# Two-layer transformer block on one core: first experts' weights split during the cross attention, attention weights' low parts in a head's first step, first head's split moved and its zeroing left out

## The chip, the core and the metric

The kernel runs on one core of a Trainium2 chip. A core has five engines that run their own instruction streams and meet on semaphores: TensorE (PE, matrix products into PSUM), VectorE (DVE), ScalarE (ACT), GpSimd (POOL) and SyncE (SP, here only a queue that issues transfers). The metric is the device time of one launch in microseconds, lower is better.

## What is computed

2048 tokens of width 256 (32 sequences of 64) pass six blocks, each with a layer norm ahead and added to the residual `x`:

```
x = x + L0_attn(norm(x))              # rotary recurrence, 6 heads
x = x + L0_xattn(norm(x), ctx, mask)  # grouped-query cross attention, 16 heads, ALiBi, mask
x = x + L0_ffn(norm(x))               # 16 routed experts, top 2, and 2 shared ones; itself x + shared + routed
x = x + L1_attn(norm(x))              # lightning attention, 16 heads of 128
x = x + L1_xattn(norm(x), ctx)        # attention with quantised q, k, v and weights
x = x + L1_ffn(norm(x))               # 16 routed experts, top 4, and a shared one
```

The cross attention takes, per head, `softmax(q k / 4 + slope * (key - query position), masked)` times `v`. An expert of L0_ffn is `w2(gelu(g x + gb) * (w1 x + b1)) + b2`. The lightning attention projects q, k, v (SiLU) and a gate (sigmoid) per head, multiplies `q k^T` with a decay that stays inside 64-token sequences here, multiplies with `v`, normalises over all heads, gates and projects out.

## The kernel before

The functions run one behind the other, each as one or a few blocks of five engine streams; a block ends when all five have ended. Tokens lie in 16 tiles of 128 (`NT`); a step of most loops handles 512 tokens (`BLK`), so four steps (`NBLK`) make a pass, of four tiles each (`TPB`). Nothing plans the order: every engine's stream is written out by hand, and semaphores tie them.

**Products in two halves.** To have near-float32 products at 16-bit speed, operands are split into a high part (`x * 1024` rounded to float16) and a low part (what the rounding left), and `split_product` (L117) runs high*high, high*low and low*high. So every weight and every activation needs a high part (an ACT instruction with `scale=SPLIT`) and a low part (a subtraction on DVE or POOL).

**`layernorm`** (L159 on). DVE computes moments, ACT the root (L221, with a load of ACT's function table ahead), DVE normalises the tiles (L205), PE turns them (L246), ACT copies them from PSUM (with `split` as high parts, L228), and DVE makes the low parts (L197). With `scalar_first` ACT does something of the caller's ahead of the root, with `gpsimd` POOL beside it all.

**`gqa_cross_attention`** (L538 on). Per block of 512 tokens PE projects queries, keys (and values from `ctxS`, a copy of the block's context that POOL makes, L598); ACT copies them out. Then four steps of one tile n: PE's scores (L704); DVE scales them and adds the bias (L658), takes the maximum (L663) and subtracts it (L664, two inputs in SBUF), ACT takes the exponential (L631), DVE sums (L679) and inverts, PE turns the weights (L752), ACT copies them (L634, two per step), PE multiplies with the values (L762), DVE divides (L684), PE turns and projects out (L722), DVE adds to X (L669). POOL makes the next bias (ALiBi plus mask, 128x1024, L602) in the one of two buffers that step n-2 has consumed: it waits for `biased >= n + 1` and nothing else.

**`experts_top2`** (L1117 on). Stage of its own (`m.stage()`): its semaphores are cleared at its end. `RowNorm` normalises on DVE (L900), adds to X (L905), ACT makes high parts (L916) and DVE low parts (L892); for each 512 tokens SP then issues a transposing transfer (L925, output in `xh` or `xl`) and a transfer that keeps the rows in DRAM. PE computes the router's logits (L117), ACT the scores (L996), and a chain of some 80 DVE instructions chooses two experts per token and places the tokens (`Dispatch`, L1009 to L1114). Then POOL gathers the rows of 12 groups of 512 places from DRAM (L1247), SP transposes them (L1214), PE runs them through their experts, ACT and DVE evacuate, the results are kept and gathered back (L1255) into `G`, and DVE combines them (L1360); the shared experts run on PE meanwhile.
The weights of the 18 experts are loaded by SP in six slots (`weights`, L1178 to L1186) and split here: ACT scales them in place (L1263, L1264) and rounds them (L1266, L1267), POOL subtracts (L1237, L1238). ACT's split of experts 0 and 1 stands ahead of the root, those of 2 to 5 between the high parts, the rest before and behind the scores. The first routed product waits for all 18 (`split`).

**`lightning_attention`** (L1501 on). Its norm is `layernorm(..., split=True, scalar_first=first_high, gpsimd=first_low)`: ACT scales head 0's weights in place and rounds them (two instructions of 128x1280, L1577 and L1579), POOL zeroes `SQ` (L1582), subtracts (L1584) and zeroes `ACC` (L1585). Then 16 heads of four steps s. In a step PE runs, for step s+1, the projections, and for step s `k q`, the previous step's output product and `A v`; ACT evacuates; DVE masks (`mask`, L1684), adds the previous output from PSUM to `ACC` (`add`, L1692), gates (L1698) and makes y's low part (L1701); POOL squares (L1604) and sums the squares in `SQ` (L1607). The next head's weights are rounded by ACT in step 0 (L1619) and subtracted by DVE behind step 1:

```
for q in range(SPH):
    s = h * SPH + q
    mask(s, h)
    if not (first and q == 0):
        add(s - 1, (q - 1) % SPH)
    gated(s, h, q)
    if q == 1 and not last:
        weights_low(h + 1)
```

SP then issues one transposing transfer of both parts (`turn`, L1559) into `T`, and the loads of the head after. PE waits for that transposition in step 3, ahead of the next head's first projection (`pe.wait_ge(wt_in, 16 * (h + 2))`).

## Time and profile before

| | us |
|---|---|
| Median of three runs | 2724.72 (2721.74 to 2728.42) |
| Profiled execution, its own time | 2709.75 |
| Its span | 2707.9 |

| Engine | busy us | share | instructions |
|---|---|---|---|
| PE | 1998.0 | 74% | 15918 |
| DVE | 1845.4 | 68% | 3197 |
| ACT | 1458.6 | 54% | 2020 |
| POOL | 1018.0 | 38% | 921 |

| Stage | from, us | to, us | granted PE clock |
|---|---|---|---|
| cross attention, steps | 279.3 | 477.9 | 0.77 |
| experts' router | 477.9 | 551.1 | 0.51 |
| experts' products, combination | 551.1 | 716.2 | 0.88 |
| norm ahead of the lightning attention | 716.2 | 744.7 | 0.56 |
| lightning attention | 744.7 | 1320.9 | 0.98 |
| quantised attention | 1320.9 | 2200.5 | 0.56 |
| top-4 experts | 2200.5 | 2707.9 | 0.96 |

Times count from the start of the span. The granted clock is a share of 2.4 GHz. Engines overlap, so busy times are no sum of anything: what counts is what each stage waits for last. The chain of waits that the page follows back from the last instruction reaches only to the start of the last stage, so earlier stages are read from time lines. In these, a line is one instruction or a run of like ones; in brackets is how long its engine had been idle, and whose work ended that.

### The profile page before, as it was taken

The numbers are of one execution on the slowest core, as the hardware profiler recorded it, in microseconds if no ns is written. First come the engines' busy times: TensorE is split into PE (matmuls) and PEld (weight loads), VectorE is DVE, ScalarE is ACT, GpSimd is POOL, SyncE is SP. The second block draws the span as 40 slices with busy tenths as digits, with TensorE's granted clock in tenths as the row PEclk, the third lists the DMA queues.
The fourth block names the chain that finished last, engine by engine and source line by source line (L and its number), as shares of the span: only waits on it lengthen the run. The fifth ranks groups of instructions, "written<-read, shape, count | busy, mean of one in ns | idle before, by whom it ended". The sixth has DMA issues, their size and how long they took to land. (4 is left out here: it accounts for less than half of the span.)

```text
span 2707.9 us, 44268 instructions
## 1 busy us (share of the span) xinstructions
PE 1998.0 (74%) x15918; PEld 1185.8 (44%) x15918; DVE 1845.4 (68%) x3197; ACT 1458.6 (54%) x2020; POOL 1018.0 (38%) x921
## 2 busy tenths in 40 slices
PE   6884777158399999999563566666666549999998
PEld 3332555146267677777452122222222324444444
DVE  5997566733645455555656999999999546666665
ACT  4662333523254444444232888888888326666664
POOL 0000221553423333333134788888888401001010
PEclk8886777579799999999776555555555659999999
DMA  3000000666311111111000556565666200000001
GB/s 93 0 0 21 1 0 0 170 147 146 82 23 37 39 39 39 39 39 30 24 0 0 102 106 108 108 106 108 107 107 108 44 19 18 17 26 17 26 17 40
DMA packets 416195, 145.93 MB, mean 54 GB/s; under 512 B 359021, under 2 KB 412997, under 8 KB 416069
## 3 DMA queue, kind: packets, MB, share of 16 engines
q1 hardware_dynamic: 412229, 133.76, 24.2%
q0 software_dynamic: 3840, 10.49, 1.7%
q8 instruction: 79, 1.29, 0.2%
q14 instruction: 47, 0.39, 0.0%
HBM read 47.69 MB, written 10.49 MB: 21 GB/s over the span
## 5 line engine op out<-in xcount | busy, mean ns | idle before, releaser
L2057 POOL CAST xnT<-xl 128x2048 bf16<-128x2048 uint8 x256 | 483.6, 1890 | 16.1 <-DMA xl<-xh 0.7
L2092 PE MATMUL psum<-e_KT,e_QT 48*128 48x512 bf16 x1024 | 265.1, 618 | 271.9 <-DVE ctxT L2125 125.1
L2125 DVE TENSOR_SCALAR_CACHE_REDUCE ctxT<-psum,e_nsq 128x1024 f32<-128x1024 f32 x256 | 314.7, 1282 | 11.8 <-PE psum L2092 10.1
L2125 DVE TENSOR_SCALAR_CACHE_REDUCE e_Smore<-psum,e_nsq 128x1024 f32<-128x1024 f32 x256 | 314.7, 1282 | 1.4
L2143 ACT ACTIVATE xh<-e_Smore,e_ebias 128x2048 uint8<-128x2048 f32 x128 | 256.3, 2002 | 48.4 <-POOL e_ebias L2064 48.4
L2143 ACT ACTIVATE xh<-ctxT,e_ebias 128x2048 uint8<-128x2048 f32 x128 | 256.3, 2002 | 47.5 <-POOL e_ebias L2064 47.5
L1604 POOL TENSOR_TENSOR d_sq<-d_oS 128x512 f32<-128x512 f32 x64 | 96.9, 1514 | 399.1 <-ACT d_oS L1653 399.1
L117 PE MATMUL psum<-xh,d_T 128*128 128x512 f16 x768 | 221.9, 385 | 22.8 <-DMA d_T<-d_Ws 19.0
L2092 PEld LDWEIGHTS psum<-e_KT,e_QT 48*128 48x128 bf16 x1024 | 33.9, 107 | 401.8 <-DVE ctxT L2125 190.4
L2281 POOL TENSOR_TENSOR f_WA<-f_W,f_WA 128x512 f16<-128x512 f32 x17 | 19.6, 1155 | 410.0 <-ACT f_W2H L2301 410.0
L2102 PEld LDWEIGHTS psum<-e_Vi,xnT 128*128 128x128 bf16 x4096 | 119.3, 104 | 112.9 <-issue 104.3
L117 PE MATMUL psum<-xh,f_WA 128*128 128x512 f16 x544 | 154.5, 387 | 13.9 <-DVEq L2336 11.8
L2352 DVE SCALAR_TENSOR_TENSOR X<-psum,f_route,X 128x256 f32<-128x256 f32 x272 | 112.8, 477 | 70.3 <-PE psum L2412 70.3
L1701 DVE SCALAR_TENSOR_TENSOR d_yl<-d_y,d_nw,d_yh 128x512 f16<-128x512 f32 x64 | 105.4, 1647 | 72.0 <-ACT d_yh L1658 72.0
L2412 PE MATMUL psum<-f_W2H,f_hh 128*128 128x256 f16 x544 | 151.1, 278 | 3.1 <-DVE f_hh L2364 3.1
L2412 PE MATMUL psum<-f_W2L,f_hh 128*128 128x256 f16 (+1 forms) x544 | 151.0, 278 | 0.0
L2102 PE MATMUL psum<-e_Vi,xnT 128*128 128x16 bf16 x4096 | 131.2, 175 | 8.1 <-POOL xnT L2057 8.1
L1628 ACT ACTIVATE d_gt<-psum 128x512 f32<-128x512 f32 x64 | 38.2, 597 | 164.1 <-PE psum L117 164.1
L2315 ACT ACTIVATE f_h<-psum 128x512 f32<-128x512 f32 x68 | 40.6, 597 | 158.0 <-PE psum L117 158.0
L2342 DVE TENSOR_TENSOR f_pr<-psum,f_h 128x512 f32<-128x512 f32 x68 | 47.0, 692 | 111.3 <-ACT f_h L2315 111.3
L1698 DVE SCALAR_TENSOR_TENSOR d_y<-d_gt,d_oS 128x512 f32<-128x512 f32 x64 | 44.3, 692 | 108.3 <-ACT d_oS L1653 108.3
L117 PE MATMUL psum<-xl,d_T 128*128 128x512 f16 x384 | 116.2, 385 | 0.0
(366 smaller groups left out, 4806.8 us busy)
## 6 DMA issues: line engine op xcount, KB each, us to landing
kept_y<-c_y SPq DMA_DIRECT2D x12, 512.0 KB, 3.7
d_Wn<-in_L_attn_w_qkv SPq DMA_DIRECT2D x16, 384.0 KB, 3.4
f_W<-in_L_ffn_w_routed SPq DMA_DIRECT2D x32, 176.0 KB, 2.5
xl<-xh SPq DMA_TRANSPOSE x256, 3.1
ctx_rows<-in_ctx SPq DMA_DIRECT2D x1, 2048.0 KB, 9.3
X<-in_x SPq DMA_DIRECT2D x1, 2048.0 KB, 14.7
c_Wgu<-in_L_ffn_rg SPq DMA_DIRECT2D x16, 128.0 KB, 2.6
c_Wgu<-in_L_ffn_rw SPq DMA_DIRECT2D x16, 128.0 KB, 2.7
```

The source lines that it names most:

```text
L117: mm = pe.matmul(out, lhsT(a, k), rhs(b, k), start=(n == 0), stop=(n == len(terms) - 1))
L1604: pool.tensor_tensor(sq[:, :], o, o, ALU.mult).then_inc(squared, 1)
L1698: dve.scalar_tensor_tensor(y[:, :], gt[:, q % 2, :], 1.0, oS[:, q % 2, :], ALU.add, ALU.mult).then_inc(yready, 1)
L1701: dve.scalar_tensor_tensor(yl[:, :], y[:, :], nw[:, ds(h, 1)], yh[:, :], ALU.mult, ALU.subtract).then_inc(ysplit, 1)
L2057: pool.tensor_copy(PT[:, sl, :], P8[:, sl, :, :].rearrange("p c q -> p (c q)").bitcast(U8)).then_inc(unpacked, 1)
L2092: mm = pe.matmul(m.bank[pair_banks(c + odd) + q], QT[rows, n // 2, :], KTt[rows, n % H // 2, col:col + BLK], start=True, stop=True)
L2102: mm = pe.matmul(m.bank[6 + j // 8][:, j % 8 * HD:(j % 8 + 1) * HD], PT[:, n % SLOTS, k // 2 * 2 * P + k % 2:(k // 2 + 1) * 2 * P:2], Vi[: ...
L2125: dve.tensor_scalar(S32[sl][:, hf * HALF:(hf + 1) * HALF].rearrange("p (a b) -> p a b", a=2), m.psum[:, b:b + 2, :], nsq[:, n + odd:n + od ...
L2143: act.activation(e8[:, sl, :], S32[sl], ACT.Exp, bias=ebias[:, sl:sl + 1], scale=-1.0, accum_out=esum[:, n:n + 1]).then_inc(exped, 1)
L2342: dve.tensor_tensor(pr[:, st % 2, 0, :], m.bank[1][:, :], h1[:, st % 2, 0, :], ALU.mult).then_inc(product, 1)
L2352: last = dve.scalar_tensor_tensor(m.X[:, t, :], m.bank[4 + 2 * (q % 2) + j // 2][:, (j % 2) * D:(j % 2 + 1) * D], R.route[:, t, ds(e, 1)], ...
L2412: mm = pe.matmul(m.bank[4 + 2 * (q % 2) + j // 2][:, (j % 2) * D:(j % 2 + 1) * D], a, b, start=(n == 0), stop=(n == len(terms) - 1))
```

## The change

- `SplitWeights` (new) holds the experts' weight slots (four), the split weights and their semaphores. The two shared experts are loaded during the cross attention's norm and split ahead of its loop; the 16 routed ones are split one per step of the loop, ACT's part behind its copies of the step, POOL's part ahead of the bias. SP reloads a slot when POOL has done with it. `experts_top2` has no weight work left. Both functions are in one `m.stage()`.
- In the cross attention the biases of tiles 0 and 1 are made ahead of the loop, and step n makes that of tile n+2; two more rows of `neg`, set to zero, stand for tiles 16 and 17, whose biases nobody reads. The copy `ctxS` moves from POOL to ACT.
- In the router ACT's second to fourth high parts stand behind the wait for the eleven small loads. The gathered results go to `m.xnT` in sixteen slots instead of eight.
- In the lightning attention's norm ACT takes the root first and then rounds head 0's weights in one instruction (`scalar_mid`); DVE makes the low part between the normalisation and the low part of the norm's second block (`vector_mid`), in one instruction for scale and subtraction. POOL has nothing there.
- `ACC` and `SQ` are not zeroed: the first four sums are copies, head 0's squares are written straight to `SQ`.
- `weights_low(h + 1)` moves from behind step 1's `gated` to the first step, between `add` and `gated`.

```
+                    if vector_mid and b == 1:
+                        vector_mid(dve)
...
-                if scalar_first:
-                    scalar_first(act)
                 act.wait_ge(moments_done, (r + 1) * (NT + 1))
                 act.activation(sd[:, :], mom[:, :, 1], ACT.Sqrt, bias=eps[:, :]).then_inc(sd_done, 1)
+                if scalar_mid:
+                    scalar_mid(act)
...
+    def load(self, sp, kind, e, slot):
+
+        for part, name in enumerate(("g", "w1")):
+            sp.dma_start(self.Wgu[:, slot, :, part, :],
+                         self.w[f"L0_ffn_{kind}{name}"][e].rearrange("(k p) f -> p k f", p=P)).then_inc(self.w_in[slot], 16)
+        sp.dma_start(self.Wd[:, slot, :], self.w[f"L0_ffn_{kind}w2"][e]).then_inc(self.w_in[slot], 16)
+
+    def scalar(self, act, e, slot, loads, n):
+
+        act.wait_ge(self.w_in[slot], 48 * loads)
+        act.activation(self.Wgu[:, slot], self.Wgu[:, slot], ACT.Copy, scale=SPLIT)
+        act.activation(self.Wd[:, slot], self.Wd[:, slot], ACT.Copy, scale=SPLIT).then_inc(self.scaled, 1)
+        act.wait_ge(self.scaled, n + 1)
+        act.activation(self.Wx[:, ds(e, 1), 0].rearrange("p o k a f -> p (o k a f)"),
+                       self.Wgu[:, slot].rearrange("p k a f -> p (k a f)"), ACT.Copy)
+        act.activation(self.WdH[:, ds(e, 1)].rearrange("p o d -> p (o d)"), self.Wd[:, slot], ACT.Copy).then_inc(self.high, 1)
+
+    def gpsimd(self, pool, e, slot, n):
+
+        pool.wait_ge(self.high, n + 1)
+        flat = lambda x: self.Wx[:, ds(e, 1), x].rearrange("p o k a f -> p (o k a f)")
+        pool.tensor_tensor(flat(1), self.Wgu[:, slot].rearrange("p k a f -> p (k a f)"), flat(0), ALU.subtract)
+        pool.tensor_tensor(self.WdL[:, ds(e, 1)].rearrange("p o d -> p (o d)"), self.Wd[:, slot],
+                           self.WdH[:, ds(e, 1)].rearrange("p o d -> p (o d)"), ALU.subtract).then_inc(self.split, 1)
...
+            for slot in range(W.SH):
+                W.load(sp, "s", slot, slot)
...
+                    sp.wait_ge(W.split, slot + 1)
+                    W.load(sp, "r", slot, slot)
+                for slot in range(W.SH, W.SLOTS):
+                    W.load(sp, "r", slot, slot)
+                with sp.Fori(1, NBLK) as i:
+                    for slot in range(W.SLOTS):
+                        sp.wait_ge(W.split, i * W.SLOTS + (W.SH - W.SLOTS + 1) + slot)
+                        W.load(sp, "r", i * W.SLOTS + slot, slot)
+
             @block.gpsimd
             def _(pool):
-                pool.wait_ge(prep, 1 + KC * C)
+                for slot in range(W.SH):
+                    W.gpsimd(pool, W.NE + slot, slot, slot)
+                pool.wait_ge(prep, 2 + KC * C)
+
+                def mask_bias(n, half):
+                    pool.wait_ge(biased, n + 1)
+                    pool.tensor_tensor(bias[:, half, :, :], alibi[:, :, :],
+                                       neg[:, ds(n, 1), :].broadcast_to((P, NH, SEQ)), ALU.add).then_inc(bias_ready, 1)
+
+                mask_bias(0, 0)
+                mask_bias(1, 1)
                 with pool.Fori(0, NBLK) as i:
-                    pool.wait_ge(proj, i * 4 + 4)
-                    pool.tensor_copy(ctxS[:, :, :], m.ctxT[:, :, ds(i * BLK, BLK)]).then_inc(ctx_copied, 1)
                     for tt in range(TPB):
-                        n = i * TPB + tt
-                        pool.wait_ge(biased, n + 1)
-                        pool.tensor_tensor(bias[:, tt % 2, :, :], alibi[:, :, :],
-                                           neg[:, ds(n, 1), :].broadcast_to((P, NH, SEQ)), ALU.add).then_inc(bias_ready, 1)
+                        W.gpsimd(pool, i * W.SLOTS + tt, tt, i * W.SLOTS + (W.SH + tt))
+                        mask_bias(i * TPB + (tt + 2), tt % 2)
...
+                    W.scalar(act, W.NE + slot, slot, 1, slot)
+                act.wait_ge(prep, 2 + KC * C)
                 with act.Fori(0, NBLK) as i:
+                    act.wait_ge(proj, i * 4 + 4)
+                    act.activation(ctxS[:, :, :], m.ctxT[:, :, ds(i * BLK, BLK)], ACT.Copy).then_inc(ctx_copied, 1)
...
+                        W.scalar(act, i * W.SLOTS + tt, tt, i + (2 if tt < W.SH else 1), i * W.SLOTS + (W.SH + tt))
...
+                dve.memset(neg[:, NT:, :], 0.0).then_inc(prep, 1)
...
-    STAGES, GOT, TURNED, GSLOTS = 6, 2, 3, 8
+    GOT, TURNED, GSLOTS = 2, 3, 16
...
-        G = norm.xn[:, :, :, :].rearrange("p a b d -> p (a b) d")
+        G = m.xnT[:, :, :].rearrange("p a b -> p (a b)").rearrange("p (s d) -> p s d", s=GSLOTS)
...
-                    for n in range(STAGES):
-                        weights(n)
...
-                split_high(0)
-                split_high(1)
                 norm.scalar_sd(act)
-                for b in range(NBLK):
-                    norm.scalar_high(act, b)
-                    split_high(2 + b)
-                split_high(STAGES)
-                split_high(STAGES + 1)
+                norm.scalar_high(act, 0)
                 act.wait_ge(loaded, 16 * NLOADS)
                 act.activation(b2[:, 0, :], b2[:, 0, :], ACT.Copy, scale=HS * SPLIT).then_inc(bias_high, 1)
                 R.scalar_gate(act, R.wa[:, :, :].rearrange("p k e -> p (k e)"))
+                for b in range(1, NBLK):
+                    norm.scalar_high(act, b)
                 R.scalar_scores(act, m.bank[6])
-                for n in range(STAGES + 2, NE + SH):
-                    split_high(n)
...
-                pe.wait_ge(split, NE + SH)
...
-            act.activation(flat(Wn[:, :, :]), flat(Wn[:, :, :]), ACT.Copy, scale=SPLIT).then_inc(wscaled, 1)
-            act.wait_ge(wscaled, 1)
-            act.activation(flat(Ws[:, 0]), flat(Wn[:, :, :]), ACT.Copy).then_inc(whigh, 1)
-
-        def first_low(pool):
-            pool.memset(SQ[:, :], 0.0).then_inc(squared, 4)
-            pool.wait_ge(whigh, 1)
-            pool.tensor_tensor(flat(Ws[:, 1]), flat(Wn[:, :, :]), flat(Ws[:, 0]), ALU.subtract).then_inc(wsplit, 1)
-            pool.memset(ACC[:, :, :], 0.0).then_inc(acc_zero, 1)
-
-        layernorm(nc, m, preload, split=True, scalar_first=first_high, gpsimd=first_low)
+            act.activation(flat(Ws[:, 0]), flat(Wn[:, :, :]), ACT.Copy, scale=SPLIT).then_inc(whigh, 1)
+
+        def weights_low(dve, h):
+
+            dve.wait_ge(whigh, h + 1)
+            dve.scalar_tensor_tensor(flat(Ws[:, 1]), flat(Wn[:, :, :]), SPLIT, flat(Ws[:, 0]), ALU.mult,
+                                     ALU.subtract).then_inc(wsplit, 1)
+
+        layernorm(nc, m, preload, split=True, scalar_mid=first_high, vector_mid=lambda dve: weights_low(dve, 0))
...
-                with pool.Fori(0, NH) as h:
+                for q in range(SPH):
+                    pool.wait_ge(ocopied, q + 2)
+                    pool.tensor_tensor(SQ[:, q * BLK:(q + 1) * BLK], oS[:, q % 2, :], oS[:, q % 2, :],
+                                       ALU.mult).then_inc(squared, 2)
+                with pool.Fori(1, NH) as h:
...
-                def add(s, q):
+                def add(s, q, fresh):
                     dve.wait_ge(outs, s + 2)
                     for half in range(2):
                         t = q * TPB + 2 * half
                         a2 = ACC[:, t:t + 2, :].rearrange("p t d -> p (t d)")
-                        last = dve.tensor_tensor(a2, m.bank[6 + half][:, :], a2, ALU.add)
+                        if fresh:
+                            last = dve.tensor_copy(a2, m.bank[6 + half][:, :])
+                        else:
+                            last = dve.tensor_tensor(a2, m.bank[6 + half][:, :], a2, ALU.add)
...
-                        if not (first and q == 0):
-                            add(s - 1, (q - 1) % SPH)
+                        if n or q:
+                            add(s - 1, (q - 1) % SPH, n * SPH + q <= SPH)
+                        if q == 0 and not last:
+                            weights_low(dve, h + 1)
                         gated(s, h, q)
-                        if q == 1 and not last:
-                            weights_low(h + 1)
...
-                dve.wait_ge(acc_zero, 1)
-                head(0, True, False)
-                with dve.Fori(1, NH - 1) as h:
-                    head(h, False, False)
-                head(NH - 1, False, True)
+                head(0, 0, False)
+                head(1, 1, False)
+                with dve.Fori(2, NH - 1) as h:
+                    head(h, 2, False)
+                head(NH - 1, 2, True)
...
+        with m.stage(), ExitStack() as split:
+            W = SplitWeights(m, w, split)
+            gqa_cross_attention(nc, m, w, W)
+            experts_top2(nc, m, w, W, kept_rows, kept_y)
...
```

## Rows read from the trace of the kernel before

**Rows 1.** Windows view, lightning attention: engines' busy us, granted PE clock, DMA share.

```profile
744.70:1320.90 576.20, 546.48 (x4512) 404.25 (x4512) 304.66 (x358) 256.32 (x420) 178.41 (x128) 0.98 0.15 33
```

**Rows 2.** Time line of DVE, cross attention: start us, us, instruction, idle before, releaser.

```profile
292.98 1.29 DVE L658 SCALAR_TENSOR_TENSOR b_S<-psum,b_bias 128x512 f32<-128x512 f32 x2 [12.15 <-PE psum L704]
...
303.27 2.32 DVE L664 TENSOR_TENSOR b_S<-b_S,b_mx 128x1024 f32<-128x1024 f32 x1
...
321.93 1.22 DVE L679 TENSOR_REDUCE b_tot<-b_S 128x16 f32<-128x1024 f32 x1 [0.46 <-ACT b_S L631]
...
461.24 1.22 DVE L679 TENSOR_REDUCE b_tot<-b_S 128x16 f32<-128x1024 f32 x1 [0.46 <-ACT b_S L631]
...
467.70 1.22 DVE L679 TENSOR_REDUCE b_tot<-b_S 128x16 f32<-128x1024 f32 x1 [0.46 <-ACT b_S L631]
```

**Rows 3.** Time lines of POOL and ACT, the same stage.

```profile
302.16 2.35 POOL L602 TENSOR_TENSOR b_bias<-b_alibi,b_neg 128x1024 f32<-128x1024 f32 x1 [5.37 <-DVE b_S L658]
...
301.02 0.60 ACT L634 ACTIVATE b_PT<-psum 128x512 f32<-128x512 f32 x1 [0.26 <-PE psum L752]
```

**Rows 4.** Split of an expert's weights: ACT time line, POOL source line (ns min/median/max).

```profile
523.08 0.61 ACT L1263 ACTIVATE c_Wgu<-c_Wgu 128x512 f32<-128x512 f32 x1
...
524.87 0.61 ACT L1263 ACTIVATE c_Wgu<-c_Wgu 128x512 f32<-128x512 f32 x1
...
L1237 POOL TENSOR_TENSOR c_Wx<-c_Wgu,c_Wx x18: 1147/1189/3194, 483.9 to 546.4; 128x512 f16<-128x512 f32 x18
```

**Rows 5.** Time lines of DVE, SP and PE, router of the first experts.

```profile
487.28 0.25 DVE L887 RECIPROCAL c_rstd<-c_sd 128x16 f32<-128x16 f32 x1 [2.67 <-ACT c_sd L912]
...
494.88 1.93 SPq L925 DMA_TRANSPOSE xh<-xnT  x1
...
506.88 3.02 SPq L925 DMA_TRANSPOSE xl<-xnT  x1
...
516.91 0.81 PE L117 MATMUL psum<-c_wa,xl 128*128 128x16 f16 x24 [1.97 <-DMA xl<-xnT]
```

**Rows 6.** Lines view of DVE, 525.8 to 550.2 us: xcount, busy us, mean ns, idle.

```profile
L1100 DVE TENSOR_TENSOR c_y<-c_iota,c_row 128x2048 f16<-128x2048 f32 x2 | 6.0, 2993 | 0.0
...
L1096 DVE TENSOR_TENSOR c_tilehot<-c_iota,c_tile 128x768 f16<-128x768 f32 x2 | 3.3, 1632 | 0.0
...
L1070 DVE TENSOR_SCALAR c_tile<-c_slot 128x32 f32<-128x32 f32 x1 | 1.1, 1137 | 0.0
```

**Rows 7.** Time lines, norms: cross attention's (270.36), then lightning attention's.

```profile
270.36 2.67 DVE L205 TENSOR_SCALAR ln_xn<-X,ln_mom,ln_rstd 128x256 f32<-128x256 f32 x8
...
721.75 1.17 DVE L188 BATCH_NORM_AGGREGATE ln_mom<-ln_stats 128x2 f32<-128x6 f32 x16
...
726.55 6.60 DVE L205 TENSOR_SCALAR ln_xn<-X,ln_mom,ln_rstd 128x256 f32<-128x256 f32 x8
...
727.24 3.51 POOL L1585 MEMSET d_ACC<- 128x4096 f32 x1
...
731.91 3.67 PE L246 MATMUL psum<-ident,ln_xn 128*128 128x128 f32 x16 [31.57 <-DVE ln_xn L205]
```

**Rows 8.** Time lines, lightning attention: PE at head boundaries, DVE in head 1.

```profile
779.14 0.61 PE L117 MATMUL psum<-xh,d_T 128*128 128x512 f16 x2 [2.02 <-DMA d_T<-d_Ws]
...
1267.64 0.61 PE L117 MATMUL psum<-xh,d_T 128*128 128x512 f16 x2 [1.22 <-DMA d_T<-d_Ws]
...
794.14 1.29 DVE L1692 TENSOR_TENSOR d_ACC<-psum,d_ACC 128x512 f32<-128x512 f32 x2 [0.51 <-PE psum L117]
...
797.13 0.69 DVE L1698 SCALAR_TENSOR_TENSOR d_y<-d_gt,d_oS 128x512 f32<-128x512 f32 x1 [1.69 <-ACT d_oS L1653]
...
805.44 0.69 DVE L1698 SCALAR_TENSOR_TENSOR d_y<-d_gt,d_oS 128x512 f32<-128x512 f32 x1 [1.69 <-ACT d_oS L1653]
...
808.85 1.48 DVE L1707 SCALAR_TENSOR_TENSOR d_Ws<-d_Wn,d_Ws 128x1280 f16<-128x1280 f32 x1
```

More of the change, by code:

```diff
@@ L535, in _, with __init__, gqa_cross_attention @@
                 output(NBLK - 1)
-def gqa_cross_attention(nc, m, w):
+class SplitWeights:
+    NE, SH, F, SLOTS = 16, 2, 128, 4
+    def __init__(self, m, w, own):
+        NE, SH, F, SLOTS = self.NE, self.SH, self.F, self.SLOTS
+        self.w = w
+        self.Wgu = m.sb("c_Wgu", [P, SLOTS, KC, 2, F], ctx=own)
+        self.Wd = m.sb("c_Wd", [F, SLOTS, D], ctx=own)
+        self.Wx = m.sb("c_Wx", [P, NE + SH, 2, KC, 2, F], F16, own)
+        self.WdH, self.WdL = (m.sb("c_" + n, [F, NE + SH, D], F16, own) for n in ("WdH", "WdL"))
+        self.scaled, self.high, self.split = (m.sem(f"c_{n}") for n in ("scaled", "high", "split"))
+        self.w_in = [m.sem(f"c_w{i}") for i in range(SLOTS)]
+    def load(self, sp, kind, e, slot):
[17 more added lines that the diff above has]
+                           self.WdH[:, ds(e, 1)].rearrange("p o d -> p (o d)"), ALU.subtract).then_inc(self.split, 1)
+def gqa_cross_attention(nc, m, w, W):
     G, C, HD = 4, 4, 16
@@ L1233, in _ @@
                 pool.memset(b2r[:, :, :], 0.0).then_inc(bias_clear, 1)
-                for n in range(NE + SH):
-                    e, slot = ORDER[n], n % STAGES
-                    pool.wait_ge(high, n + 1)
-                    pool.tensor_tensor(Wx[:, e, 1], Wgu[:, slot], Wx[:, e, 0], ALU.subtract)
-                    pool.tensor_tensor(WdL[:, e], Wd[:, slot], WdH[:, e], ALU.subtract).then_inc(split, 1)
                 pool.wait_ge(norm.kept, 16 * NBLK)
@@ L1716, in finish, with head @@
                         dve.scalar_tensor_tensor(m.X[:, t, :], ACC[:, t, :], rstd[:, t:t + 1], m.X[:, t, :], ALU.mult, ALU.add)
-                def head(h, first, last):
+                def head(h, n, last):
                     for q in range(SPH):
```

69 lines of the change are left out of this document (16 added, 53 removed).

## Prediction

> **What bounds the kernel now.** The program is seven stages one behind the other, so I read the busy times by stage first, then the time lines of the stages that the diff touches, for what each waits on last. In the lightning attention TensorE (PE) is busy 546 of 576 us at nearly full clock [rows 1]: only idle time of PE can be won there. The cross attention is a ring of VectorE (DVE), ScalarE (ACT) and PE, some 7.6 us a step, but 6.46 us (461.24 to 467.70) in the last ones, where GpSimd (POOL) has nothing left to do [rows 2]. The router of the first experts is a DVE chain with SyncE's (SP's) transpositions in it [rows 5, 6], and the norm ahead of the lightning attention waits for DVE [rows 7].
>
> **What one lock does.** POOL's bias ran from 302.16 to 304.51 [rows 3]; DVE's subtraction, asked for at 303.27, took 2.32 us [rows 2], which is the remaining 1.24 us plus the 1.22 us that 1024 elements take (the sum at 461.24 [rows 2]), less some overlap. So a DVE instruction with two SBUF inputs and a POOL instruction exclude each other. DVE's reductions and its reads of PSUM did not stretch. All terms below use this.
>
> **1. Cross attention, given 18 expert splits.** One split is 1.79 us of ACT (523.08 to 524.87) and 1.81 us of POOL: 1.15 for 512 elements [rows 4] and 0.66 at that rate for the down part's 256. ACT's copies end at 301.62 [rows 3] and its next exponential waits for the subtraction that ends at 305.59 [rows 2]: 4.0 us free, which cover the 1.79 (without them, every step would pay 1.79). The context copy that ACT takes over, at most 1.2 us by the 0.60 of half its size [rows 3], comes while PE still computes the block's queries. The six loads ahead of the stage ride on SP behind those of the norm; the later ones have a whole block each. The DVE memset of 128 elements is 0.1 us by size. POOL's order changes: bias n+2 now stands behind split n, and split n behind the exponentials' transposed copies on ACT. Worked through a block of four steps, from its first score:
> - step 0: POOL is idle at the first subtraction, so that takes 1.22, not 2.3 us: 1.1 us gained.
> - step 1: ACT's copies ended 1.65 us before the subtraction began [rows 2, 3]; plus 1.79, POOL's split is ready 0.15 us after that start, waits for its 1.22, runs 1.81, then the bias 2.35 [rows 3]: ready 5.4 us after the start. DVE wants it after 3.9 (1.22 plus exponential, sum and reciprocal). So 1.1 us gained, 1.5 lost.
> - steps 2 and 3: the subtraction meets one half of the split instead of the bias, about 0.4 to 1 us, and the bias is just about in time.
> The sum is 27.4 us from first score to last exponential, against 28.95 now (292.98 to 321.93 [rows 2]): -1.55 in three blocks. In the last block two subtractions already run free, 26.7 (28.95 less twice 1.1), and would now meet POOL: +0.7. Together **-4.0**. No row shows the new interleaving; its bounds are -15, fourteen stretches of 1.1 gone and no bias late, and +20, the first rival. I take the value worked out, since one lock at a time is what rows 2 and 3 show.
>
> **2. Router.** The 72 ACT and 36 POOL instructions of the splits leave. (a) The square root stood behind two splits and a table load: DVE waited 2.67 us for it [rows 5]; some 0.35 remain, -2.3. With POOL quiet DVE then needs 1.34 us for four normalisations (2.67 for eight [rows 7]), 1.2 each for the addition and the low part, so the first low part ends at 491.6 where its transposition is now issued at 494.88 [rows 5]: -3.3. From there to the last landing at 516.91 [rows 5] are 22.0 us, with six weight loads on SP just ahead of the third transposition at 506.88 [rows 5]. Without them and with DVE's spacing of 3.7, 3.7, 3.7 and 1.2 us the landing comes at 508.5: **-8.4**. Bounds: -6.8, where the transfers keep their present spacing less 3.5 us for six issues, and -8.9, where they follow DVE at once; I take the inner value because the transfer engines then carry nothing else. ACT now waits for the eleven small loads ahead of the second high part; they are the first things that SP issues, from 478 on at about half a microsecond each, and are wanted at 489. If they came late, everything above would slip by as much.
> (b) Behind the scores DVE works 24 us beside POOL's splits. The two of 2048 elements took 2.99 each [rows 6]; free they take 2.28 (0.69 us for 512 [rows 8] and 1.22 for 1024 [rows 2] give 1.04 ns an element): -1.4. The two of 768 took 1.63, free 0.96: -1.35. A 32-element operation took 1.14 [rows 6] and needs 0.18 by the same line: -0.96. Seven more groups of that view by the same comparison: -4.9. Together **-8.6** (bounds -4.5 and -9.5). The gathers, the routed loop (PE waiting on transposed rows) and the combination keep their lengths and shift; sixteen gather slots for eight are worth 0.5 us of POOL waits at most, taken as 0. Router: **-17.0**.
>
> A page can be held against (a): "DMA: Bandwidth & Descriptors" of the Trainium skill, section Latency and other measured facts, gives a transposition 261 GB/s, by estimate 2.0 us for a block's 512 KB; the blocks would then follow DVE's low parts directly, and the term would be -17.5. No row here isolates it.
>
> **3. Norm ahead of the lightning attention.** Moments are ready at 722.92, but the first of eight normalisations begins at 726.55, behind two ACT passes over the head's weights and a table load [rows 7]. Afterwards the root comes first and they begin at 723.6: -3.0. They then took 6.60 us because POOL's split and the zeroing of 3.51 us ran to 730.75; free, eight take 2.67 [rows 7]. The first transposition starts at 731.91 [rows 7] and would start at 725.0: **-6.9**. The moved low part (1.48 us on DVE [rows 8]) runs from 726.35 to 727.85, before the first PSUM low part can start at 728.2, and the weights' transposition is issued 0.5 us later than now against a start of PE that comes 6.9 earlier: by my estimate 3 us are left. ACT's one pass instead of two fits behind the root. The two memsets cost nothing except as lockers. Bounds -3.0 (only the earlier start) and -7.5.
>
> **4. Low part in a head's first step.** Now it is made in the second step, at 808.85 [rows 8], and PE waits for the transposition at every head boundary. From the stall before 779.14 to the one before 1267.64 [rows 8] are 488.5 us for fourteen heads; steps within a head are 8.31 us (797.13 to 805.44 [rows 8]), so 56 steps are 465.4: 23.1, plus the first stall's 2.02: **-25.1**. This includes the boundaries where PE resumed at the lower clock. One step earlier is 8.3 us, more than the 2.02 of the first stall and the 1.22 of the last [rows 8]. The price is DVE's place between the addition, which ends at 795.43, and the gate at 797.13 [rows 8]: 1.70 us free for 1.48, so nothing, with 0.2 us to spare. ACT's high part is made in that same first step already, ahead of the gate's input, and SP's transposition and three loads move forward with the low part. If ACT's part were late, DVE would wait ahead of the gate, and PE's output product behind it. PSUM copies instead of additions in the first four sums and POOL's single multiplication in head 0 run beside PE. Bounds: -25.5, and -4 if all DVE time is paid (second rival).
>
> **Sum:** -4.0 - 17.0 - 6.9 - 25.1 = -53.0 us. The profiled execution took 2709.75 us (2656.8 after); the median of the runs is 2724.72, 15 us above it, spread over stages that I can't see; I put the difference on the median: 2671.7 us.
>
> **Rivals.**
> - *POOL's instructions in a row keep DVE out until all are through.* For it: the eight normalisations of 6.60 us lost both POOL instructions in turn [rows 7]. Then subtractions 2 and 3 wait 4 us, a block grows by 4.5 us and the last by 6.7: +20 instead of -4, total -29: 2696. Against it: DVE waited for one bias only. 12%. The Trainium skill's "SBUF — State Buffer", section Who interferes with whom, says that whichever instruction starts first holds the shared ports for its whole length and the other blocks: by that the wait is one instruction, and the forecast stands. By that rule, the trace agrees on 303.27.
> - *The low part ahead of the gate delays it*: the 0.2 us are not there, and 1.4 us are paid at fifteen heads: -53 + 21, 2693. Against it: PE has its own work queued. 8%.
> - *The router's transfers were the bound*: only the contention term and the first 3.3 us come, -48: 2677. 5%.
> - *Slower: the lightning attention, no longer interrupted, loses PE's granted clock.* A step of 8.31 us would take 16.6 at 1.2 GHz; from about 7.4 such steps on the 53 us are gone and 8.2 more. For it: the stalls are PE's only pauses. Against it: 0.98 of full clock over the stage as it is, 95% busy [rows 1]. 2%; at ten steps 2755.
> - The change does not do what it says (the bias chain binds each step, no stall disappears): 1%.
>
> **Chances.** The forecast 72%. 0.3% is 8.2 us, about what a measurement of this kernel can tell from no change. The range: downward the bounds added as independent ones give -64, nearly all of it the cross attention's, and the runs differ by some 3 us, 2658; upward it takes in the terms' own bounds and the third rival and stops at the second, -33, leaving the first out: 2692. Faster 0.95, within 0.3% 0.03, slower 0.02.
>
> **What would show it.** After: DVE's normalisation in one run of 2.7 us in the third norm and no POOL work beside it; no wait of PE for the weights' transposition, heads of 33.2 us; scores 8 us and token list 17 us nearer to the router's start; in the cross attention stretched subtractions of at most about 2.4 us and waits for the bias in step 2 of a block. Wrong would be: a step over 8 us there, a PE wait for the low part of y in first steps, a transposition that still lands 22 us after the first, or a clock below 0.95 in the lightning attention.

## The result, and where the time went

The changed kernel takes 2679.58 us (median of 4 runs, 2676.91 to 2685.68) against 2725.01 (4 runs, 2721.74 to 2728.42): 0.983 of before, 95% interval 0.9812 to 0.9848, or -45.4 us. Forecast were 2671.7 us, 2658 to 2692. The sum of the terms is another matter, and the traces take it apart. Each row of this table is the distance between two marks on DVE's time line (its first instruction of a stage, the reading of the token list, the end of a stage's last addition into `X`), for the first profile of each kernel and for one more of each (a2 and a1 below):

| stretch, us | before | before, again | after | after, again |
|---|---|---|---|---|
| ahead of the cross attention's second norm | 263.2 | 261.3 | 262.8 | 263.7 |
| cross attention, from that norm | 214.9 | 214.9 | 208.0 | 208.0 |
| router, to the token list | 71.9 | 72.7 | 54.7 | 55.0 |
| experts' products and combination | 161.0 | 176.2 | 191.2 | 191.3 |
| gap to the next norm | 5.4 | 5.4 | 1.4 | 1.4 |
| norm ahead of the lightning attention | 28.3 | 27.8 | 21.4 | 21.5 |
| lightning attention | 576.2 | 574.4 | 555.0 | 555.4 |
| the rest | 1387.0 | 1387.1 | 1384.9 | 1384.3 |
| span | 2707.9 | 2719.6 | 2679.5 | 2680.5 |

Router and norm moved as forecast, the cross attention by more, and the experts' products, taken as unchanged, grew by 15 to 30 us. In no other profile of either kernel was this stretch as short as the 161.0 us of the first one of before; this is most of why the two first spans differ by only 28.4 us and the medians by 45.4.

**Cross attention.** The time line of DVE and POOL in step 1 of the first block of after (start us, us, instruction, idle before):

```profile
301.49 1.16 POOL L573 TENSOR_TENSOR c_Wx<-c_Wgu,c_Wx 128x512 f32 x1 [12.38 <-ACT c_WdH L567]
301.85 1.87 DVE L730 TENSOR_TENSOR b_S<-b_S,b_mx 128x1024 f32<-128x1024 f32 x1
302.60 1.65 POOL L574 TENSOR_TENSOR c_WdL<-c_Wd,c_WdH 128x256 f32 x1
304.21 2.36 POOL L655 TENSOR_TENSOR b_bias<-b_alibi,b_neg 128x1024 f32<-128x1024 f32 x1
306.70 1.29 DVE L724 SCALAR_TENSOR_TENSOR b_S<-psum,b_bias 128x512 f32<-128x512 f32 x2 [0.35 <-POOL b_bias L655]
```

The subtraction, asked for at 301.85, gets its 1.22 us once POOL's first half ends at 302.65. POOL's second half, next in its row, then waits for DVE: 1.65 us instead of the 0.66 by size. The lock goes to and fro, one instruction at a time. The bias is late, as worked out, but by 0.35 us here and by 1.46 to 1.49 in two steps of each later block; DVE's waits of the whole stage have one new row:

```profile
DVE b_S L724 <- POOL b_bias L655: 9.2, 7, 1.5
```

From first score to last sum a block takes 27.66, 27.60, 27.60 and 27.59 us, against 28.95, 28.92, 28.97 and 26.67 before: -3.1 in all, by hand -4.0. The other 4 us lie in the tails, where PE ends a block. The windows view over the start of the tails of blocks 1, 2 and 3 (granted clock is the last but two), first before, then after:

```profile
323.40:333.00 9.60, 8.87 (x45) 6.91 (x45) 1.31 (x4) 2.30 (x4) 0.00 (x0) 0.50 0.01 2
372.80:382.00 9.20, 8.47 (x49) 6.73 (x48) 1.12 (x3) 2.80 (x5) 0.00 (x0) 0.56 0.00 0
421.80:431.00 9.20, 8.37 (x43) 6.57 (x44) 1.29 (x4) 2.25 (x4) 0.00 (x0) 0.50 0.00 0
```

```profile
321.80:327.10 5.30, 4.76 (x44) 3.94 (x45) 1.24 (x4) 4.00 (x8) 4.48 (x4) 1.00 0.28 77
365.40:374.50 9.10, 8.37 (x48) 6.69 (x47) 0.95 (x4) 5.02 (x10) 4.09 (x3) 0.55 0.15 43
413.10:422.00 8.90, 8.17 (x48) 6.63 (x47) 0.94 (x3) 4.83 (x10) 4.09 (x3) 0.53 0.16 44
```

The same 44 or so matmuls keep PE busy for 8.2 to 8.9 us where the granted clock was at or near the lower level (0.50 to 0.56; 1.2 GHz) and for 4.8 at the full one (1.00; 2.4 GHz). The steps, shifted against the clock, met it in full once.

**Router.** SyncE's transpositions in after (the second number is what issuing one took on SyncE's queue, not the transfer), and PE's wait for the last:

```profile
484.31 2.06 SPq L991 DMA_TRANSPOSE xh<-xnT  x1
488.12 3.11 SPq L991 DMA_TRANSPOSE xh<-xnT  x1
491.94 3.41 SPq L991 DMA_TRANSPOSE xl<-xnT  x1
496.02 3.63 SPq L991 DMA_TRANSPOSE xl<-xnT  x1
```

```profile
501.43 0.81 PE L117 MATMUL psum<-c_wa,xl 128*128 128x16 f16 x24 [3.29 <-DMA xl<-xnT]
```

From first issue to last landing are 17.1 us, before 22.0 [rows 5]; the scores are complete 8.2 us nearer to the stage's start, forecast 8.4. Behind them the lines view of DVE has the group at its free size where before had 2993 and 1632 ns [rows 6]:

```profile
L1166 DVE TENSOR_TENSOR c_y<-c_iota,c_row 128x2048 f16<-128x2048 f32 x2 | 4.6, 2284 | 0.0
...
L1162 DVE TENSOR_TENSOR c_tilehot<-c_iota,c_tile 128x768 f16<-128x768 f32 x2 | 1.9, 956 | 0.0
```

That chain gave 9.0 us (forecast 8.6). The first three transpositions are issued within 0.1 us of DVE's low parts; the fourth, whose low part is ready at 493.05, only at 496.02, behind the third and its store. What held the transfers shows in the windows view from the first issue to the last landing, before and after (the last two numbers are the DMA engines' busy share and GB/s):

```profile
494.88:516.91 22.03, 2.09 (x72) 2.00 (x73) 14.37 (x22) 10.98 (x21) 10.00 (x11) 0.50 0.95 224
```

```profile
484.30:501.40 17.10, 2.26 (x72) 2.08 (x72) 10.53 (x22) 3.40 (x3) 0.00 (x0) 0.50 0.99 226
```

The DMA engines are full in both, at the same rate. By rate and length they moved some 4.9 MB before and 3.9 MB after, and at 225 GB/s this difference is worth about the 4.9 us that the stretch became shorter: the experts' weights no longer travel among the transpositions and the stores of the rows. From the first issue on the scores wait for these transfers, not for SyncE's issues or DVE's spacing. Over 485.6 to 488.0 only the first transposition's packets ran, at 208 GB/s with the engines full, and it landed 4.4 us after its issue. The Trainium skill, "DMA: Bandwidth & Descriptors", Latency and other measured facts, has 261 GB/s, by estimate 2.0 us for a block's 512 KB: this trace does not agree, by 208 GB/s they are 2.5 us.

**Norm ahead of the lightning attention.** The root first, then eight normalisations in 2.67 us, then the low part, all ahead of DVE's first PSUM low part; no POOL instruction beside them. Before, they began at 726.55 and took 6.60 [rows 7]. 6.9 us, as forecast:

```profile
724.67 0.31 ACT L221 ACTIVATE ln_sd<-ln_mom,ln_eps 128x16 f32<-128x16 f32 x1 [5.34 <-DVE ln_mom L188]
725.30 2.67 DVE L205 TENSOR_SCALAR ln_xn<-X,ln_mom,ln_rstd 128x256 f32<-128x256 f32 x8
727.89 1.48 DVE L1602 SCALAR_TENSOR_TENSOR d_Ws<-d_Wn,d_Ws 128x1280 f16<-128x1280 f32 x1
```

**Heads.** DVE's time line where a head's first step now holds the low part:

```profile
785.17 1.29 DVE L1716 COPY d_ACC<-psum 128x512 f32<-128x512 f32 x2 [0.62 <-PE psum L117]
786.37 1.48 DVE L1602 SCALAR_TENSOR_TENSOR d_Ws<-d_Wn,d_Ws 128x1280 f16<-128x1280 f32 x1
788.05 0.69 DVE L1724 SCALAR_TENSOR_TENSOR d_y<-d_gt,d_oS 128x512 f32<-128x512 f32 x1 [0.19 <-ACT d_oS L1676]
```

The gate still waits 0.19 us for ACT: these are the 0.2 us to spare that were forecast. PE's waits for the weights' transposition, 19.0 us in 15 pieces before, are gone: the waits view of PE over the stage has three rows, and none is a DMA. The windows view of the stage, against [rows 1]:

```profile
739.56:1294.57 555.01, 544.98 (x4512) 407.00 (x4512) 303.98 (x358) 256.50 (x420) 174.85 (x124) 0.98 0.15 35
```

Steps take 8.3 us throughout, and the 63rd step's gate comes 24.9 us earlier, counted from the stage's start (530.85 us against 555.74; forecast 25.1), or 23.1 against the second profile of before (553.96). The last step then takes 13.08 us instead of 9.32. What changed there, PE's 24 small matmuls for the first twelve tiles' norms, in before and in after:

```profile
1305.32 2.74 PE L1775 MATMUL psum<-d_ones,d_SQ 128*128 128x1 f32 x24
```

```profile
1275.72 5.12 PE L1796 MATMUL psum<-d_ones,d_SQ 128*128 128x1 f32 x24
```

Between the last steps PE idles for 2 us in both; in after the granted clock is down to 0.50 from about 1275 on, in before only from 1310. So the stage gave 21.1 us and not 24.9.

**Experts' products.** PE's waits by `issue` (it waited for nothing that the profile shows) over this stretch, before and after:

```profile
PE psum L1419 <- issue: 8.9, 10, 1.3
PE psum L117 <- issue: 0.2, 1, 0.2
```

```profile
PE psum L117 <- issue: 16.8, 26, 1.4
PE psum L1441 <- issue: 7.1, 10, 1.3
```

A sample from the shared products of after, PE and POOL: single matmuls some 0.7 or 1.4 us apart, for 16 us, while POOL issues one gather every 1.25 us without a pause. POOL stops at 681.4, and the stall ends 3 to 4 us later:

```profile
669.21 0.95 POOL L1292 DMA_INDIRECT xnT<-kept_y,c_home  x1 [0.30 <-issue]
670.08 0.27 PE L1443 MATMUL psum<-c_WdH,c_hl 128*128 128x256 f16 x1 [0.99 <-issue]
670.46 0.95 POOL L1292 DMA_INDIRECT xnT<-kept_y,c_home  x1 [0.30 <-issue]
670.79 0.27 PE L1444 MATMUL psum<-c_b2r,c_ones_bf 128*128 128x256 bf16 x1 [0.45 <-issue]
671.50 0.27 PE L1441 MATMUL psum<-c_WdH,c_hh 128*128 128x256 f16 x1 [0.44 <-issue]
...
680.48 0.95 POOL L1292 DMA_INDIRECT xnT<-kept_y,c_home  x1 [0.30 <-issue]
```

My theory was that PE's instructions come late while POOL issues gathers, and that sixteen slots, which let it issue twenty in a row, made it worse. The rivals: chance from run to run, or the code's new place. One row of the first profile of before already speaks against the simple form of this theory. There POOL issued all 32 gathers in a row, some 1.25 us apart:

```profile
668.21 0.95 POOL L1255 DMA_INDIRECT c_xn<-kept_y,c_home  x1 [31.47 <-DMA kept_y<-c_y]
...
707.68 0.94 POOL L1255 DMA_INDIRECT c_xn<-kept_y,c_home  x1 [0.30 <-issue]
```

and over 660 to 715 us, the shared products' part, PE has no wait by issue, only this row:

```profile
PE psum L1419 <- DVE c_hl L1334: 4.1, 3, 1.4
```

### The profile page after: what moved, and what is told of

Its sections match the earlier page's. It is cut to its first block and busy times, and to the rows that moved or that the text cites. A ratio compares the mean times of both kernels' runs of the same rounds, so it can differ in the third digit from the quotient of the medians.

```text
span 2679.5 us, 44374 instructions
## 1 busy us (share of the span) xinstructions
PE 2002.0 (75%) x15918; PEld 1190.3 (44%) x15918; DVE 1813.6 (68%) x3199; ACT 1461.2 (55%) x2023; POOL 1005.3 (38%) x912
## 5 line engine op out<-in xcount | busy, mean ns | idle before, releaser
L2302 POOL TENSOR_TENSOR f_WA<-f_W,f_WA 128x512 f16<-128x512 f32 x17 | 19.7, 1157 | 407.5 <-ACT f_W2H L2322 407.5
L573 POOL TENSOR_TENSOR c_Wx<-c_Wgu,c_Wx 128x512 f32 (+1 forms) x18 | 26.0, 1445 | 385.1 <-ACT c_WdH L567 385.1
```

## The experiments

### Both kernels once more (a1, a2)

No edit.

> The changed kernel, unaltered, for a second profile. In its first profile the first experts' products and combination (token list ready to the last addition into X) took 191.0 us against 160.8 before, with TensorE idle in pieces of some 0.7 us that no wait explains. Theory (the stalls are instruction delivery and differ from run to run): this stretch has another length here, anywhere from 160 to 190 us, and the span moves with it. Rival (the change itself lengthens it, by its sixteen gather slots or by the placing of its code): 191 us again, within 3 us. Time 2680 us, 0.983 of before, in both.

> The kernel before, unaltered, for a second profile. Its first profiled execution was 15 us faster than the median of its runs. Theory (run-to-run stalls in the first experts' products): this stretch takes 165 to 180 us instead of 160.8, and the span is some 2720 us. Rival (the stretch is fixed in each kernel): 161 us again and a span of 2708 us.

a1: 2676.09 us, 0.9811 of before (0.9788 to 0.9834), products and combination 191.3 us. a2: 2721.39 us in one run, 176.2 us. The stretch of after repeats within 0.1 us, so its growth is not chance: the rival held there. That of before moves by 15 us between two profiles: there the theory held.

### The change in two halves (a3, a4)

a3 is before with the hunks of the norm helper and the lightning attention; a4 is before with all the others.

> Only the last two parts of the change: the norm ahead of the lightning attention, and a head's low part in its first step with the first head's other engines. Prediction's terms: -6.9 and -25.1, less the 3.8 us that the clock took back at the lightning attention's end in the first profile of after: -28 to -32 us, 2693 to 2697 us. Rival (the parts help one another): less than 25 us.

> Only the first parts: the experts' weights split in the cross attention, the router without them, the gathers' sixteen slots. Prediction's terms: -4 and -17, and -3.4 measured besides in the first profile of after at the cross attention's and the stage's ends: -24 us, 2701 us. Rival (the change lengthens the experts' products by up to 30 us): between -24 and +6, the remainder of what a3 leaves of the whole -45: -13 to -17 us.

a3: 2698.69 us, 0.991 (0.9893 to 0.9928), -26.5 us, a little less than the 28 to 32 expected, though its last step took 9.32 us, the clock falling late as in before; a4's did too, so neither half's profile has the 3.8 us. a4: 2705.43 us, 0.9929 (0.9908 to 0.9949), -19.7 us: between the theory's 24 and the rival's 17. Products and combination took 184.8 us in a4 and 178.8 in a3. The halves add up to -46.2; the whole gave -45.4 in its first runs and -49.1 in those of a1.

### The gathers' slots (b1, b2)

```diff
-    GOT, TURNED, GSLOTS = 2, 3, 16
+    GOT, TURNED, GSLOTS = 2, 3, 8
-        G = m.xnT[:, :, :].rearrange("p a b -> p (a b)").rearrange("p (s d) -> p s d", s=GSLOTS)
+        G = norm.xn[:, :, :, :].rearrange("p a b d -> p (a b) d")
```

b1 is after with this edit, b2 is before with its reverse.

> The changed kernel with eight slots for the combination's gathers (in the norm's buffer, as before) in place of sixteen. Theory (TensorE's instructions come late while POOL issues gathers back to back, and sixteen slots let it issue twenty in a row): products and combination take 165 to 180 us instead of 185 to 191, no stall of TensorE of over 10 us in the shared products; time 2665 to 2672 us against 2676 to 2680. Rival (the slots have nothing to do with it): 185 to 191 us and 2680 us. Second rival (sixteen slots save POOL's waits, as intended): longer by 1 to 5 us.

> The kernel before with sixteen slots in place of eight, and nothing else. Theory (as for b1): products and combination take 180 to 190 us in place of the 161 to 179 of the profiles so far, with one stall of TensorE of 15 us or more in the shared products; 2730 to 2740 us. Rival: as before, 2725 us.

b1: 2670.80 us, 0.9802 (0.9785 to 0.9819); products and combination took 179.7 us, as expected. b2: 2727.85, 1.0017 (1.0005 to 1.0029), 5.0 us longer, so at the edge of what was expected; the stretch took 183.0 us. What they did is read best from the four additions of the shared products into X, here in b1:

```profile
654.93 1.29 DVE L1371 SCALAR_TENSOR_TENSOR X<-psum,X 128x512 f32<-128x512 f32 x2 [0.27 <-issue]
669.42 1.28 DVE L1371 SCALAR_TENSOR_TENSOR X<-psum,X 128x512 f32<-128x512 f32 x2
679.63 1.29 DVE L1371 SCALAR_TENSOR_TENSOR X<-psum,X 128x512 f32<-128x512 f32 x2 [0.27 <-PE psum L1444]
694.61 1.29 DVE L1371 SCALAR_TENSOR_TENSOR X<-psum,X 128x512 f32<-128x512 f32 x2 [7.46 <-remote]
```

First to fourth addition, in the profiles with gathers beside these products: sixteen slots 48.9, 48.2, 48.2, 47.4, 48.4 and 49.7 (after, a1, a4, b3, b4, c3) and 48.4 in b2, whose stage is otherwise that of before; eight slots 39.7, 39.3, 36.9 and 39.3 (b1, a2, a3, c1), and 28.0 in the first profile of before alone. So the slots cost some 9 us or more here, in either kernel, and the rest of the growth is not theirs. On the whole stage it is less: with sixteen the gap to the next norm is 1.3 to 1.4 us, with eight 5.4 to 5.6. Between the profiles of after and b1 3.7 us more lie in the last step of the lightning attention, which took 9.32 us in b1.

### All gathers behind the products (c2)

```diff
                 for sl in range(2):
                     pool.wait_ge(kept[sl], 16 * (QUADS // 2))
+                pool.wait_ge(summed, NBLK)
```

and DVE's additions of the gathered rows all behind its last shared addition.

> The changed kernel with all 32 gathers of the combination, and all its additions, behind the last shared product. Theory (the stall of TensorE in the shared products comes of the gathers that POOL issues beside them): no piece of TensorE idle by issue in that part; the last addition of a shared product comes 13 to 18 us earlier than in the two profiles of after, where it is bound by the stall. The whole is longer all the same, since 32 gathers take 40 us: products and combination 210 to 220 us. Rival (instruction delivery at that place of the code is slow whatever POOL does): the stall of 13 to 18 us is there, with no gather beside it.

```profile
653.89 1.29 DVE L1372 SCALAR_TENSOR_TENSOR X<-psum,X 128x512 f32<-128x512 f32 x2 [0.27 <-PE psum L1441]
662.57 1.29 DVE L1372 SCALAR_TENSOR_TENSOR X<-psum,X 128x512 f32<-128x512 f32 x2 [0.27 <-PE psum L1441]
671.24 1.29 DVE L1372 SCALAR_TENSOR_TENSOR X<-psum,X 128x512 f32<-128x512 f32 x2 [0.28 <-PE psum L1441]
678.70 1.29 DVE L1372 SCALAR_TENSOR_TENSOR X<-psum,X 128x512 f32<-128x512 f32 x2 [2.02 <-PE psum L1441]
```

24.8 us from first to fourth, half of after's 48.9. PE's waits over 650 to 683 us are a single row, and not by issue:

```profile
PE psum L1438 <- DVE c_hl L1357: 1.2, 1, 1.2
```

The stall is gone with the gathers beside it. The last addition comes 31 us sooner than in after (678.70, 709.52): 24.1 of these lie between the four additions, where 13 to 18 were expected, 5.9 between the token list and the first, where c2 changes only the last 4 us (the first gathers), and 0.9 ahead of that. So without the gathers, and without DVE's additions of the gathered rows, which moved with them, there is no stall; the two were not told apart. The first profile of before, with 32 gathers in a row and no stall, shows that gathers back to back are not enough for one: what else it takes is open. So is how it comes about. The DMA view of after over the stall, 669 to 684.5 us, has one queue only, the gathers' own:

```profile
q0 software_dynamic: 532, 1.44, 32.3%
```

No packet of an instruction queue was under way then (the view lists these as kind `instruction`), and the DMA engines were a third full; before, over 672 to 701 us, they were 0.36 full with no stall. So a slow transfer of instructions through these engines is not seen; some other way by which they come late is only argued. The stretch took 198.3 us, less than the 210 expected, since 40 us of gathers follow products that are shorter: 2687.24 us in one run.

### Order of bias and split on POOL (b3), and the splits' own cost (c3)

```diff
-                        W.gpsimd(pool, i * W.SLOTS + tt, tt, i * W.SLOTS + (W.SH + tt))
                         mask_bias(i * TPB + (tt + 2), tt % 2)
+                        W.gpsimd(pool, i * W.SLOTS + tt, tt, i * W.SLOTS + (W.SH + tt))
```

> The changed kernel with POOL's bias ahead of its split in each step of the cross attention. The bias is then asked for when the subtraction of the same step is through and is ready 2.4 us later; the split of 1.8 us follows beside DVE's sums. Theory (the late bias in steps 2 costs some 3 us in all): cross attention 1 to 3 us shorter than the 207.0 and 208.0 us of the two profiles of after (from its second norm's start), its subtractions stretched as before instead. Rival (the split behind the bias stretches the next subtraction and delays the experts' loads): 0 to 6 us longer.

> The changed kernel, where the experts' splits in the cross attention handle 8 elements of each part, and the rest of the split weights is zero, written by POOL behind the last step. The loads, the order and every wait stay. It tells what the splits themselves cost there. Theory (the split's 1.8 us on POOL is what delays the bias and stretches the subtractions): no wait for a bias, the first subtraction of a block stretched or the next free, blocks of 42 to 44 us as with the bias first: cross attention 9 to 13 us shorter than in after. Rival (waits and order cost it, the split's length nothing): blocks of 47.7 us again.

b3: 2669.20 us, 0.9786 (0.9762 to 0.9809). The cross attention took 196.4 us instead of 208.0: 11.6 gained where 1 to 3 were expected. No wait for a bias is left. But from first score to last sum the four blocks take 107.3 us instead of 110.4, 3.1 gained. That this meets the expectation is in part luck: three blocks gained 1.3 to 1.9 us each, while the third took 28.97 us at a granted clock of 0.66, where d1, with the same order, took 25.61 at 0.81 (below; its four blocks took 103.7). The other 8.5 are tails, three of four at full clock, where after has one of four:

```profile
321.10:326.80 5.70, 4.84 (x44) 3.94 (x45) 1.29 (x4) 4.40 (x9) 3.14 (x3) 1.00 0.26 73
363.20:371.50 8.30, 7.46 (x44) 6.00 (x45) 1.03 (x4) 4.81 (x9) 3.14 (x3) 0.59 0.32 95
411.40:417.00 5.60, 4.98 (x45) 4.00 (x46) 1.31 (x4) 4.32 (x9) 3.36 (x3) 1.00 0.27 75
453.90:459.80 5.90, 4.23 (x42) 3.37 (x42) 1.32 (x5) 2.68 (x8) 3.09 (x4) 1.00 0.00 0
```

c3 leaves out nearly all of the splits, so the experts work with zeros. Its 2686.19 us (one run) and the 219.6 us of its cross attention hold POOL's zeroing of the split weights behind the last step and can't be compared; the blocks can: the blocks' pitch is 44.07, 44.04 and 44.85 us against 43.69, 47.74 and 47.76, which looks like the theory. It is not. From first score to last sum the blocks take 27.93, 27.95, 28.53 and 27.88, no less than with the full splits: the waits for the bias went, and the earlier bias met the subtractions instead (31.2 us for the sixteen, 21.0 in after). All three tails were at full clock, which is the whole of the shorter pitch. In this order the splits' work costs nothing that shows: they keep the bias out of the subtractions' way for what they delay it.

### The low part in the second step (b4)

```diff
-                        if q == 0 and not last:
-                            weights_low(dve, h + 1)
                         gated(s, h, q)
+                        if q == 1 and not last:
+                            weights_low(dve, h + 1)
```

> The changed kernel with a head's low part in the head's second step, as before; the first head's other engines stay. Theory (prediction, step 4): TensorE waits at each head boundary again, steps 0 to 62 of the lightning attention take 553.5 to 556 us instead of 530.9, and the tail is 3.8 us shorter again since the clock falls later: +20 us on the whole, 2697 us. Rival (other engines in head 0 carry part of the gain): +10 to +15 us.

2695.35 us, 0.9893 (0.9877 to 0.9909): 16 to 19 us above after's 2679.6 and 2676.1. Steps 0 to 62 took 551.3 us instead of 530.9, and PE waits for the transposition at all 15 boundaries again, 17.9 us in all. So the moved low part is worth 20.4 us; the last step took 9.32 us again. The 551.3 lie below the expected 553.5 and below the 553.3 to 555.7 of the profiles with the old first head, so 2.0 to 4.4 us of the heads' term may be the first head's; those profiles differ by 2.4 us among themselves, most of it in the first three steps, which leaves that open.

### Both edits, and four slots (c1, d1)

> The changed kernel with both edits that shortened it: POOL's bias ahead of its split in each step of the cross attention, and eight slots for the combination's gathers. If the two are independent: the cross attention 196 us from the second norm's start as in b3, products and combination 165 to 180 us as in b1, 2658 to 2664 us (2678 less 7 to 10 and 6 to 9), 0.977 of before. Rival (they share one cause, the position at which code and gathers meet): no better than b3, 2669 us.

> c1 with four slots for the combination's gathers. It has the same code otherwise. Theory (each run of gathers that POOL issues without a pause costs TensorE instructions for about as long as it lasts beyond the first ones, 20 in a row at sixteen slots, 12 at eight): 8 in a row at four slots, the stall in the shared products under 5 us, but POOL waits for the additions more often: products and combination 175 to 190 us, 2653 to 2668 us, no clear difference from c1's 2659.6. Rival (with four slots the gathers' own 2 to 3 us from issue to landing bind, one group behind the other): 195 to 210 us, 2675 us or more.

c1: 2659.57 us, 0.9751 (0.9737 to 0.9764), better than both kernels and as the sum of the two edits foretold (products and combination 183.8 us, a little over the range). d1: 2662.74, 0.978 (0.9756 to 0.9803), 183.8 us: the shared products shrank once more, 35.5 us from first to fourth addition, and POOL's waits took it back. Eight and four slots can't be told apart by the time.

## Why the prediction was right, and where it was not

- **Cross attention, -4.0: measured -6.9.** Inside the blocks -3.1, with the late bias of about 1.5 us that was worked out (not in the first block, and in step 3 too from the second on, where it was taken to be just in time). The 4 us of the tails were not in the sum: they are PE's clock, which no term looked at.
- **Router, -17.0: measured -17.2.** The sizes held, -8.2 and -9.0. The reason given for the first did not: "the transfer engines then carry nothing else" was read as room to spare, and the term was priced by SyncE's issues and DVE's spacing. The engines were full before (0.95) and are after (0.99); what the term gained from first issue to last landing, 4.9 us, is about what the 1.1 MB less to move take, read from the two windows and not tested by a run of its own. That the size came out is luck in this part.
- **"The gathers, the routed loop ... and the combination keep their lengths and shift; sixteen gather slots ... taken as 0": failed.** The slots were priced as waits of POOL (0.5 us); with them the shared products take 9 us more of PE's time or more, in either kernel, and without gathers beside them the stall is gone. From the token list to the first shared addition the stretch is 122.4 to 131.4 us in four profiles with the old stage and 129.3 to 135.9 in ten with the new one; PE's waits by issue, added up, are 9.0 to 17.0 us there in the old and 13.6 to 20.0 in the new. The cause of these some 5 us is open. On the other side the gap to the norm shrank from 5.4 to 1.4 us, because the additions, not POOL's last gather, now end the stage.
- **Norm, -6.9: measured -6.9.**
- **Heads, -25.1: measured -24.9 up to the last step**, of which 20.4 are the moved low part by b4, and +3.8 in it by the clock in both profiles of after. b3 and d1 had that loss too, c3 a part of it (10.97 us), a3, b1, c1 and c2 not, all with the same code in this stage: what decides it is open.
- **Base.** The sum was set on the median, 15 us above the profiled execution, as "spread over stages that I can't see". It was in one place: the products' stretch, which took 161.0 us in that execution and 176.2 in the next. The terms alone, against the two second profiles (2719.6 and 2680.5), gave -39 and not -53. That the total came within 8 us is luck as much as the terms' merit: the median as base gave back what the missed stretch cost.
- **Rivals.** *POOL's instructions in a row keep DVE out* is refuted by 301.85, where DVE comes in between two of them. The low part does not delay the gate (0.19 us of idle time is left). *The router's transfers were the bound* did not come as priced, since the 22.0 us from first issue to last landing became 17.1, but its reading was right: the transfers bind there in both kernels. The lightning attention kept 0.98 of full clock.

## What to carry to other kernels

- A buffer that only decouples can cost time elsewhere: sixteen slots for eight took 9 us of PE's time here. Look for PE idle by issue, in single matmuls, and at what POOL issues then; measure fewer slots before more.
- Read the DMA engines' busy share over a run of transfers before its spacing is put down to the queue that issues them: at 0.95 and more, bytes are what to take away.
- In a stage at part clock, read a gain in two parts: work that DVE or ACT sets, and tails of PE, which took 1.7 to 1.8 times as long at the lower clock here. A changed order can move the second by more than the first (8.5 and 3.1 us in b3), so a gain is no proof of the reason for the edit.
- Profile the old kernel twice before a sum is set on one execution.

## What was not expected of the hardware

- While POOL issued indirect gathers 1.25 us apart, PE ran single matmuls 0.7 or 1.4 us apart with nothing to wait for, up to 16 us long; without them (c2), and in one profile with them (the first of before), the same products took 7.5 to 8.7 and 8.7 to 10.2 us from one addition to the next. The DMA engines were far from full: their mean busy share over 657 to 710 us was 0.28.
- The lock between DVE and POOL works both ways: in c3 a bias of 2.36 us took 3.43, while DVE's subtraction beside it kept its 1.23. The Trainium skill, "SBUF — State Buffer", Who interferes with whom, has it so (the one that starts first holds the ports for its whole length). By that rule, the trace agrees on both.
